# A graph network kernel: adjacency's weights on ACT, batched addresses and place loads, and loops that go round four laps at a time

## The reference

```python
gate = jax.nn.silu(edge_attr @ F1W + F1b) @ F2W + F2b
gate = gate + (ei * (ej @ adapt)).sum(-1, keepdims=True)
msg = gate * h[dst] * (cw * mj)[:, None]
agg = jax.ops.segment_sum(msg, src, num_segments=N)
...
for i in range(L):                      # L = 4
    qi = Q[src]; kj = K[dst]
    score = (qi * kj).sum(-1) + 0.1 * (edge_attr * qi[:, :RBF]).sum(-1) + logm[dst]
    smax = jax.ops.segment_max(score, src, num_segments=N)
    es = jnp.exp(jnp.minimum(score - smax[src], 20.0))
    ...
    aggi = jax.ops.segment_sum(alpha[:, None] * m, src, num_segments=N)
...
# third layer, ten steps (the second is like it, with degrees for weights)
msg = f[src] * edge_weight[:, None]
agg = jax.ops.segment_sum(msg, dst, num_segments=n)
...
# fourth layer
msg = h2[src, rel_type] * norm
agg = jax.ops.segment_sum(msg, dst, num_segments=inputs.shape[0])
```

## Time and profile before

| | us |
|---|---|
| median of 3 runs | 11,525.92 (11,525.92 to 11,526.84) |
| the profiled execution | 11,507.11 |
| its span | 11,505.3 |
| adjacency | 2,343 |
| gate pass | 637 |
| one attention pass, of four | 785 |
| the scans and copies behind a pass | 61 in the gate |
| both propagations | 1,427 |
| relation pass | 1,212 |

### The profile page before, as it was taken

One profiled execution on the slowest core, in us unless ns is written; L12 is line 12 of the kernel. 1 busy time (PEld: TensorE's weight loads), 2 busy tenths in 40 slices (PEclk: granted clock), 3 DMA queues, 4 the chain that ended last, 5 costly groups with the idle time before them and its releaser, 6 DMA issues. The chain is left out here.

```text
span 11505.3 us, 328287 instructions
## 1 busy us (share of the span) xinstructions
PE 8060.2 (70%) x107650; PEld 6419.3 (56%) x107651; DVE 6381.7 (55%) x21371; ACT 3299.7 (29%) x11512; POOL 4649.4 (40%) x6184
## 2 busy tenths in 40 slices
PE   2999943234777588499599769949967889962323
PEld 1777732223555477499489659938963444443323
DVE  6444453335999767688678958868872010011112
ACT  3222211112333233266256536626640000010000
POOL 0777767775000166255145415514530000026665
PEclk9999985555767699799699879969988999955555
DMA  7222223334777699399279649928957889801112
GB/s 293 59 59 59 59 59 79 72 81 120 222 223 222 179 292 311 101 248 248 71 215 248 177 111 248 248 60 226 247 141 294 356 343 372 354 24 18 18 18 18
DMA packets 2228522, 1954.48 MB, mean 170 GB/s; under 512 B 1472897, under 2 KB 1871505, under 8 KB 2189698
## 3 DMA queue, kind: packets, MB, share of 16 engines
q1 hardware_dynamic: 1872642, 1712.86, 48.6%
q10 hardware_dynamic: 252000, 173.83, 4.9%
q0 software_dynamic: 103712, 65.58, 3.8%
HBM read 1478.99 MB, written 470.93 MB: 169 GB/s over the span
## 5 line engine op out<-in xcount | busy, mean ns | idle before, releaser
L1615 POOL TENSOR_TENSOR s_rest<-s_msg 128x196 f32<-128x196 f32 x1488 | 764.3, 514 | 2232.9 <-ACT s_msg L1597 1821.5
L2104 POOL DMA_INDIRECT l_row<-H,l_rec x816 | 786.9, 964 | 2158.9 <-DMA l_rec<-REC 1839.1
L1214 PE MATMUL s_gotd<-m_table_d,s_hot 128*128 x17856 | 1423.5, 205 | 201.1 <-DMA s_hot<-OHT 193.4
L1597 ACT ACTIVATE s_msg<-s_gotd,s_es 128x49 f32<-128x49 f32 x5952 | 1310.0, 304 | 48.7 <-ACT s_es L1590 0.5
L1214 PE MATMUL s_small<-m_table_s,s_hot 128*128 x17856 | 1301.6, 185 | 0.7 <-issue 0.2
L1214 PEld LDWEIGHTS s_gotd<-m_table_d,s_hot 128*128 128x128 bf16 x17856 | 1030.8, 96 | 399.0 <-issue 233.4
L846 DVE SCALAR_TENSOR_TENSOR a_acc<-a_acc,m_keep,a_sums 128x256 f32<-128x256 f32 x1488 | 707.2, 475 | 807.8 <-remote 751.6
L455 POOL DMA_INDIRECT REC<-rec,place x800 | 949.8, 1187 | 322.7 <-issue 215.1
L746 POOL DMA_INDIRECT REC<-m_meta,m_place x800 | 951.0, 1189 | 294.9 <-issue 243.6
L791 PE MATMUL a_ptr<-m_ident_bf,a_hd 128*128 128x128 bf16 x1488 | 295.0, 275 | 1094.3 <-DVE a_hd_weighted L832 756.0
L1648 DVE TENSOR_REDUCE s_tops<-s_mt 128x512 f32 (+1 forms) x1488 | 1014.7, 682 | 2.0 <-PE s_mt L1558 1.7
(11 more groups left out here) (414 smaller groups left out, 19900.6 us busy)
## 6 DMA issues: line engine op xcount, KB each, us to landing
s_hot<-OHT SPq DMA_DIRECT2D x1488, 384.0 KB
p_row<-ADJ SPq DMA_DIRECT2D x288, 1600.0 KB
ADJ<-a_acc SPq DMA_DIRECT2D x1488, 128.0 KB
s_rec<-REC SPq DMA_DIRECT2D x1488, 98.0 KB
OHT<-a_turned ACTq DMA_DIRECT2D x372, 384.0 KB
g_hot<-OHT SPq DMA_DIRECT2D x372, 384.0 KB
REC<-fill SPq DMA_DIRECT2D x124, 624.0 KB, 10.2
g_rec<-REC SPq DMA_DIRECT2D x372, 108.0 KB
```

The source lines that it names most:

```text
L1214: last = nc.tensor.matmul(out, hot, table[k][:, bass.ds(at, w)], start=(k == 0), stop=(k == 2))
L1597: last = nc.scalar.activation(msg[:, b % KEPT, j], gotd[b % KEPT][:, j, SW:2 * SW], ACT.Copy, scale=es[:, b % 2, j:j + 1])
L1615: nc.gpsimd.tensor_tensor(rest[:, b % KEPT].rearrange("p g w -> p (g w)"), msg[:, b % KEPT].rearrange("p g w -> p (g w)"), upper(msg[:, b ...
L2104: nc.gpsimd.indirect_dma_start(out=row[:, b, j], out_offset=None, in_=table, in_offset=bass.IndirectOffsetOnAxis(ap=rec[:, b, j, GIDX - NO ...
```

## The change

Four things.

In adjacency the weighted tile is made by ACT from `hd` with a per-partition scale, four activations a turn, ahead of the copy of the transposed tiles. PE's products wait for it by a new semaphore, `s_weighted`, and so does the load of records; DVE's one-hots of destinations now count up `s_hot`.

`laps` puts four laps into the body of the loop. What doesn't divide goes to the turns written out: in gate and attention 36 turns are written out and the loop goes round 7 times over 48 turns, in relation 12 and 8 times over 24.

The batched addresses are used in the turns written out as well.

`add_groups` loads the block ends four at a time, among the scans.

```diff
+LAPS_A_TURN = 4
...
                 def load(n, b, first):
                     if not first:
-                        act.wait_ge(s_hot, n - 3)
+                        act.wait_ge(s_weighted, n - 3)
...
+                def weighted(n, b, first):
+                    act.wait_ge(s_hot, n + 1)
+                    for j in range(G):
+                        last = nc.scalar.activation(hd_weighted[:, b % 2, j], hd[:, b, j], ACT.Copy,
+                                                    scale=rec[:, b, j, W - CW:W - CW + 1])
+                    last.then_inc(s_weighted, 1)
...
-                in_turns(act, [(load, 0), (widen, 2), (store_turned, 3)], SLOTS)
+                in_turns(act, [(load, 0), (widen, 2), (weighted, 2), (store_turned, 3)], SLOTS)
...
                 def products(n, b, first):
                     pe.wait_ge(s_wide, n + 1)
+                    pe.wait_ge(s_weighted, n + 1)
...
-                in_turns(dve, [(sources, 0), (add_up(0), 2), (destinations, 0), (add_up(1), 2), (weighted, 0),
-                               (add_up(2), 2), (add_up(3), 2)], SLOTS)
+                in_turns(dve, [(sources, 0), (add_up(0), 2), (destinations, 0), (add_up(1), 2), (add_up(2), 2), (add_up(3), 2)], SLOTS)
...
+    total = count // slots
     start = -(-(most + slots) // slots)
+    start += (total - start) % LAPS_A_TURN
     for n in range(slots * start):
         turn(n, n % slots, None)
-    with engine.Fori(start, count // slots) as i:
-        for b in range(slots):
-            turn(slots * i + b, b, i)
+    with engine.Fori(0, (total - start) // LAPS_A_TURN) as i:
+        for k in range(LAPS_A_TURN):
+            for b in range(slots):
+                turn(i * (slots * LAPS_A_TURN) + (slots * (start + k) + b), b, i * LAPS_A_TURN + (start + k))
...
-def first_places(pe, mem, n, values):
+def first_places(pe, mem, values):
...
-    if not isinstance(n, int):
-        for j in range(2):
-            for base in mem["table_d_at"]:
-                pe.to_reg(at[j] * 2 + base)
+    for j in range(2):
+        for base in mem["table_d_at"]:
+            pe.to_reg(at[j] * 2 + base)
...
+    last = []
     for w in range(SW):
         ch.note(v.tensor_tensor_scan(parts[:, w], carry, parts[:, w], 0.0, ALU.mult, ALU.add))
+        if w % 6 == 2 and len(last) < NB:
+            c = len(last)
+            _, at = nc.values_load_multi_w_load_instructions(
+                mem["last"][0:1, c:min(c + G, NB)], engines=[dve.engine], min_val=0, max_val=NG - 1,
+                skip_runtime_bounds_check_because="tile_tables counts the groups of a block")
+            last += list(at)
     dve.wait_ge(ch.sem, ch.base + ch.n)
     for c in range(NB):
-        at = nc.vector.value_load(mem["last"][0:1, c:c + 1], min_val=0, max_val=NG - 1)
-        ch.note(v.tensor_copy(mem["sums"][:, c], parts[:, :, bass.ds(at, 1)].rearrange("p w o -> p (w o)")))
+        ch.note(v.tensor_copy(mem["sums"][:, c], parts[:, :, bass.ds(last[c], 1)].rearrange("p w o -> p (w o)")))
```

More of the change, by code:

```diff
@@ L723, in adjacency @@
         s_second = [room.sem(f"s_second{b}") for b in range(4)]
+        s_weighted = room.sem("s_weighted")
         s_hs, s_wide, s_hot, s_ptr, s_sums, s_turned, s_acc, s_init = (
@@ L825, in destinations @@
                     for j in range(G):
-                        v.tensor_scalar(hd[:, b, j], mem["iota_bf"][:], column(b, j, DL), None, ALU.is_equal)
-                def weighted(n, b, first):
-                    if past(n, 2):
-                        dve.wait_ge(s_sums, n - 1)
-                    for j in range(G):
-                        last = v.tensor_scalar(hd_weighted[:, b % 2, j], mem["iota"][:], column(b, j, DL),
-                                               column(b, j, W), ALU.is_equal, ALU.mult)
+                        last = v.tensor_scalar(hd[:, b, j], mem["iota_bf"][:], column(b, j, DL), None, ALU.is_equal)
                     last.then_inc(s_hot, 1)
@@ L1171, in load_places, with other_places @@
     return values
-def first_places(pe, mem, n, values):
+def first_places(pe, mem, values):
     first = pe.snap(values[0] >> 11)
     at = [v.with_bounds(min_val=0, max_val=(NB - 1) * DW) for v in (first, *values[1:])]
-    if not isinstance(n, int):
-        for j in range(2):
-            for base in mem["table_d_at"]:
-                pe.to_reg(at[j] * 2 + base)
+    for j in range(2):
+        for base in mem["table_d_at"]:
+            pe.to_reg(at[j] * 2 + base)
     return at
-def other_places(pe, mem, n, values, at):
+def other_places(pe, mem, values, at):
     s = pe.snap(values[0] - at[0] * FIRST).with_bounds(min_val=0, max_val=(NB - 1) * SW3)
-    if not isinstance(n, int):
-        for j in range(2, G):
-            for base in mem["table_d_at"]:
-                pe.to_reg(at[j] * 2 + base)
-        for base in mem["table_s_at"]:
-            pe.to_reg(s * 2 + base)
+    for j in range(2, G):
+        for base in mem["table_d_at"]:
+            pe.to_reg(at[j] * 2 + base)
+    for base in mem["table_s_at"]:
+        pe.to_reg(s * 2 + base)
     return at + [s]
-def places(nc, pe, mem, n):
-    values = load_places(nc, mem, n)
-    return other_places(pe, mem, n, values, first_places(pe, mem, n, values))
 def spots(nc, mem, n):
@@ L1307, in addresses @@
                 def addresses(n, b, lap):
-                    at[b] = other_places(pe, mem, n, at[b], first_places(pe, mem, n, at[b]))
+                    at[b] = other_places(pe, mem, at[b], first_places(pe, mem, at[b]))
                 def gathers(n, b, lap):
@@ L1534, in first_addresses @@
                         pe.to_reg((n - 3) * 2 + tops_at)
-                    at[b] = at[b], first_places(pe, mem, n, at[b])
+                    at[b] = at[b], first_places(pe, mem, at[b])
                 def other_addresses(n, b, lap):
-                    at[b] = other_places(pe, mem, n, *at[b])
+                    at[b] = other_places(pe, mem, *at[b])
                 def gathers(n, b, lap):
```

## The result

The changed kernel takes 11,947 us (median of 4 runs, 11,932 to 11,963) where the kernel before takes 11,526: a ratio of 1.036, with an interval from 1.0345 to 1.0381. The forecast was 11,640 us, in a range up to 11,930. It had the sign, and less than a third of the size.

The account below looks back on a forecast made before the run. It took DVE to bound adjacency's second half and PE to be busiest in attention. Loops with written-out turns +200 (attention) and +15 (gate), place loads -60, weights -40: +115 us, 11,640 us, range 11,340 to 11,930.

Parts of the forecast that it names:

- attention's rounds, 28: Attention loops: a four-lap round takes 107 us against 95.8, +11.2 each, seven rounds a pass, +78 us a pass.
- gate's rounds, 7: Gate loop: a four-lap round takes 83 us against 78, +5 each, +35 us over seven rounds.
- batched addresses in the 36 turns: Turns written out ahead of the loops: -28 us in each attention pass, -20 in the gate.
- place loads: Copies after the scans: loads hidden among scans, copies 0.25 us apart, -12 us five times, -60 us.
- What bounds the kernel, and that code is fetched: DVE bounds adjacency's second half, PE is busiest in attention; a lap's code stays, a four-lap body's is fetched every round.
- rival 1: PE's loops: the longer body's code stays or comes in time, so the kernel is faster, 11,245 us; chance 0.13.
- The price of a packet: PE's loops: 5.1 us per 16 KB of instructions fetched in attention, 5.2 in the gate; upper end 5.4.
- The branch back: End of each round: the branch goes to code no longer there, 5 us, with ends of 1 and 10.
- Rival 3: Loops: DVE and ACT lose code too, stalls not coinciding with PE's, 10 us more a round, 11,940 us; chance 0.10.
- Weights on ACT: Adjacency's second half: ACT becomes the bound at 4.02 us a turn against 4.19, -40 us over 274 turns.
- the first half doesn't move, its pace is not DVE's: Adjacency's first 1195 us, under POOL's scatters: DVE busy only 419 us, so moving weights changes nothing there, 0 us.
- Relation: Relation loop: a lap end on POOL costs only register steps between gathers 0.30 us apart anyway, so 0 us.

Follow-up runs that it names:

- The three sizes: The changed kernel with two, three and four laps to a loop body: 1.061, 1.043 and 1.041 of the kernel before on like chips.
- the light loads: The changed kernel with attention loops loading one tile's one-hots of four, so its output is not the reference's: 11,754.9 us, 1.020 of the kernel before.
- The one-lap kernel: The changed kernel with one lap to a loop body instead of four, everything else of the change kept: 10,412.7 us, 0.981 of the kernel before.

## Why the prediction was wrong

The forecast's terms, and what the two traces of the first chip show for each:

| term | forecast | measured |
|---|---|---|
| attention's rounds, 28 | +312 | +481 |
| gate's rounds, 7 | +35 | +91 |
| batched addresses in the 36 turns | -132 | -112 |
| place loads | -60 | -78 |
| adjacency | -40 | +43 |
| sum (with +3 at the nodes' start) | +115 | +428 |

The first three rows are counted by PE's gathers, with the cut at the first gather of the 37th turn.

**What bounds the kernel, and that code is fetched:** right. The body of 20 packets did not stay, a round's branch back went to code that wasn't there, and PE stood for 5.2 us in the mean where 5 had been taken. All of rival 1 that concerns staying is out. Its other half, that packets come in time, is nearly true once the loads are light (2.09 us a turn), and false under this kernel's.

**The price of a packet, the step that failed first.** The first laps gave 5.25 us, and the forecast took 1 us a lap off them for the pipeline filling up and used 5.1, with 5.4 as the upper end. The three sizes give 5.4, and the inside of the rounds 5.4 to 5.6: the deduction was wrong, and 20 x 0.3 = 6 us a round went with it. In the gate 5.2 was used and 5.7 measured; its window showed a DMA share of 1.00 in the loop, and the light loads show that the loads count, which the forecast had not weighed.

**The branch back.** The stand was right, but a round loses more at its branch than the stand. Size against size it is 7 us in both passes, by the inside of the rounds 6.7 and 6.0 on the first chip. A round also fetches one or two packets more than its body holds, and PE comes back at a lower granted clock (0.68); what each adds was not taken apart. Together attention's round is +18 where it had +11.2, and the gate's +13.8 where it had +5. The forecast also counted seven branches back a pass where there are six, as the last round doesn't go back. With that, the loops cost 481 + 91 = 572 us where 347 were forecast: 225 of the 313 us missed.

**Rival 3** gave 11,940, which is nearly the time, but by luck and a wrong way: DVE's and ACT's code does go (485 packets), their stands fall into PE's, and PE's code alone makes the loss.

**Batched addresses:** right, and some 4 us a pass less than forecast. From a pass's first gather to that of the 37th turn it is 80.5, 83.9, 79.9 and 79.9 us in the four passes, against 104.5 to 105.1 before: -21 to -25 where -28 was forecast, inside its ends; the gate -17 against -20. The one-lap kernel bears it out: 38 to 41 us less a pass, of which 15.6 are the copies'. The -29 and -23 that stand in that kernel's expectation took a whole round, branch and all, off a first round that has nothing to come back from.

**Place loads:** right, and a little more: copies are 0.12 us apart (3.03 for 25), not 0.25, so -15.6 us each.

**Weights on ACT, the second step that failed.** That ACT would be the bound in the second half was right. Two numbers were off. The four activations take 1.17 us and not 1.02: their starts are 0.29 us apart (1.27 for four, one alone 0.39), where those of 49 numbers in the earlier trace rows are 0.19 apart (0.88 for four, one alone 0.31). The 79 columns more cost 0.10 each, not 0.06. The way from the copy to the next widening is 2.44 us and not 2.35. So ACT's turn is 4.24 with the lap end, not 4.02, and 274 turns give +14 instead of -40. And "the first half doesn't move, its pace is not DVE's" was false: that no engine sets the pace does not mean that a step put into its chain is free. The turns made there fell from 99 to 93 in the two first traces (ACT x198 at two a turn, x556 at six), and from 128 to 109 on the other chip of the first kind, at 4.2 us each; why is open.

**Relation:** 0, as forecast (1212.1 and 1211.6 us).

## What to carry to other kernels

Before a loop's body is made longer, count the instruction records of its longest engine. Where the body stays, going round fetches nothing. Where it doesn't, every packet of it comes again in every round, with a stand at the branch on top, and a bound engine pays for the branch, and for the packets too when it uses its code up faster than they come. So a larger body is better than a middling one (1.041 against 1.061), and neither is as good as one that stays (0.981). When work is moved from a bound engine to one with slack, move as much as levels the two: all of it made ACT what DVE had been, half of it was the fastest version on both kinds of chip (0.977 of before, with one lap, batched addresses and place loads). And an engine's idle time doesn't promise that a step put on it is free: here one put on an engine that was busy a quarter of the time cost up to 20 turns.

## What the runs showed of the hardware

- PE kept a loop of 6.5 packets (1662 records) and fetched one of 7.5 in every round; of 7.0 packets both were seen, in one kernel with the same body four times.
- A round that is fetched takes 1 to 2 packets more than its body holds: 21 or 22 for 20, 9 for 7.0.
- Where a packet's code is 4.8 us of PE's work, it takes 5.4 to 5.6 us in attention under full loads. Where it is 12 us, nine packets and the branch add 4.6 to 6.7 us together.
- At a branch back to code that has gone DVE alone stands for 3.1 to 4.6 us. PE stands for 3.8 to 6.5 us, 5.0 to 5.2 in the mean, in bodies of two, three and four laps under full loads, and 4.4 in the mean with light ones.
- Chips differ: under POOL's indirect scatters adjacency made 277 turns in 1195 us on one and 99 on another, with the same kernel, the scatters themselves taking 950 us on both. It is 750 us of 11,500, more than any edit here is worth, and one of them, the weights on ACT, is a gain of 21 us on one kind and a loss of 90 on the other.
- Two waits in a row on one semaphore left one instruction record, 0.11 us long.
